# Column tiles for the attention scores of a cross-attention and expert kernel, with the value products moved behind them

## The reference, cut to what matters

```python
q = _ln(linear(ln_out, wq)).reshape(b, s, g, hpg, d)     # g = 8 groups, hpg = 2 heads each, d = 128
k = _ln(linear(ln_out, wk)).reshape(b, s, g, d)
v = linear(ln_out, wv).reshape(b, s, g, d)
scores = einsum('bsghd,btgd->bghst', q, k) * scale       # s = t = 64
core = einsum('bghst,btgd->bsghd', softmax(scores), v)
...                                                      # the same again with qx and with kx, vx of the context
out = einsum('bsi,oi->bso', quantized(concat(core, xout)), wproj)
x = x + out
x = x + experts(layernorm(x))
```

## Time and profile before

| | |
|---|---|
| median of 3 runs | 983.66 us (979.86 to 983.66) |
| span of the profiled execution, first to last instruction | 978.1 us |
| granted TensorE clock, mean | 0.996 |
| attention steps: scores at line 372 | 36.9 to 657.2 us |
| busy over the span: TensorE, VectorE, ScalarE, GpSimd | 97%, 82%, 75%, 47% |

### The profile page before, as it was taken

One profiled execution on the slowest core, in us unless ns is written; L12 is line 12 of the kernel. 1 busy time (PEld: TensorE's weight loads), 2 busy tenths in 40 slices (PEclk: granted clock), 3 DMA queues, 4 the chain that ended last, 5 costly groups with the idle time before them and its releaser, 6 DMA issues.

```text
span 978.1 us, 21551 instructions
## 1 busy us (share of the span) xinstructions
PE 946.2 (97%) x7240; PEld 674.7 (69%) x7240; DVE 798.2 (82%) x1720; ACT 736.5 (75%) x1370; POOL 458.5 (47%) x673
## 2 busy tenths in 40 slices
PE   5699999999999999999999999999999999999997
PEld 2476777777777777777777777776655566666665
DVE  6889999999999999999999999989799754444443
ACT  6988888888888888888888888865556645555554
POOL 5335655455465555555564655541036703333333
PEclk9999999999999999999999999999999999999999
DMA  9924201010001000100100010211558733343223
GB/s 220 330 73 87 44 23 55 23 47 26 28 29 45 28 28 23 49 29 22 50 23 28 28 45 28 72 65 55 182 166 241 232 114 50 50 70 57 44 29 38
DMA packets 36747, 70.35 MB, mean 72 GB/s; under 512 B 3617, under 2 KB 24737, under 8 KB 36513
## 3 DMA queue, kind: packets, MB, share of 16 engines
q1 hardware_dynamic: 27184, 54.39, 17.6%
q0 software_dynamic: 9456, 14.59, 8.8%
HBM read 55.52 MB, written 18.68 MB: 76 GB/s over the span
## 4 chain that ended last, share of the span: by engine, by line
PE 82%; DVE 9%; ACT 4%; issue 2%; POOL 1%; DMA 1%; POOLq 0%; DVEq 0%; ACTq 0%
PE b_pj L346 23%; PE b_sc L372 10%; PE b_tr L362 8%; PE b_o L401 7%; PE b_acc L444 5%; PE b_pj L1337 5%; PE b_o L1372 5%; PE b_o L1464 3%; PE b_pt L391 3%; PE b_tr L1337 3%; PE b_sc L1337 3%; PE b_pj L1417 2%; PE b_pt L1361 2%; PE b_sc L1417 1%; PE b_tr L1417 1%
## 5 line engine op out<-in xcount | busy, mean ns | idle before, releaser
L698 POOL TENSOR_TENSOR root<-vareps,neghalf 128x4 f32<-128x4 f32 (+1 forms) x128 | 174.2, 1361 | 10.0
L691 POOL TENSOR_TENSOR var<-ssq,unit 128x4 f32<-128x4 f32 (+1 forms) x128 | 54.4, 425 | 253.4 <-DVE ssq L524 253.4
L346 PE MATMUL b_pj<-w_hi,xq 128*128 128x512 f16 x384 | 147.9, 385 | 1.1 <-DVE xq L680 0.9
L346 PE MATMUL b_pj<-w_lo,xq 128*128 128x512 f16 x384 | 147.5, 384 | 0.0
L456 ACT ACTIVATE sq<-b_pj 128x512 f32<-128x512 f32 x192 | 114.9, 598 | 38.0 <-PE b_pj L346 35.0
L524 DVE TENSOR_REDUCE ssq<-sq 128x4 f32<-128x512 f32 x192 | 130.2, 678 | 9.4 <-ACT sq L456 9.4
L535 DVE TENSOR_TENSOR nrm<-raw,rstd 128x512 f32<-128x512 f32 x192 | 128.3, 668 | 1.6 <-POOL rstd L702 1.2
L372 PEld LDWEIGHTS b_sc<-kT,qT 128*128 128x128 f32 x1024 | 121.7, 192 | 6.1 <-ACT qT L483 1.7
L1313 POOL DMA_INDIRECT out<-xn x39 | 60.6, 1554 | 133.5 <-ACT xn L1543 124.0
L372 PE MATMUL b_sc<-kT,qT 128*128 128x64 f32 x1024 | 122.5, 273 | 0.7 <-ACT qT L483 0.7
L362 PE MATMUL b_tr<-ident,nrm 128*128 128x128 f32 x768 | 116.4, 274 | 6.8 <-DVE nrm L535 3.6
(11 more groups left out here) (327 smaller groups left out, 2271.7 us busy)
## 6 DMA issues: line engine op xcount, KB each, us to landing
nst<-in_ffw SPq DMA_DIRECT2D x40, 512.0 KB, 3.7
wload<-in_ffw SPq DMA_DIRECT2D x20, 512.0 KB, 4.5
xbuf<-zero SPq DMA_DIRECT2D x13, 387.0 KB, 9.7
xn<-xbuf SPq DMA_DIRECT2D x9, 516.0 KB, 3.7
x_sb<-in_x SPq DMA_DIRECT2D x4, 512.0 KB, 13.8
wproj<-in_ctxT SPq DMA_DIRECT2D x1, 2048.0 KB, 10.3
xhl<-in_w_all SPq DMA_DIRECT2D x4, 512.0 KB, 17.4
wproj<-in_wprojT POOLq DMA_DIRECT2D x4, 512.0 KB, 6.3
```

Of the source, the lines that this page charges most:

```text
L346: last = pe.matmul(o, x, w[kind][:, k, at:at + BANK], start=(k == 0 and n_ == 0), stop=(k == KT - 1 and n_ == len(terms) - 1))
L698: pool.tensor_tensor(root[:, r % 2, c, :], vareps[:, r % 2, c, :], neghalf[:, 0:1].unsqueeze(2).to_broadcast(shape), ALU.pow).then_inc(s[" ...
```

## The change

Each score product is split by head: 64 stationary columns of `qT` instead of 128, with the result on the partitions of that head (0 to 63 or 64 to 127) of the same columns of `b_sc`. A step has 16 such products instead of 8. In TensorE's list `pe_values` moves from behind the second transposes to the place right behind the scores. `pe_values` gets one more wait, in its first step only, for the last of the 32 weight units.

```diff
@@ pe_scores
                 for g in range(GU):
                     for b in range(2):
-                        last = pe.matmul(b_sc[:, (g * 2 + b) * S:(g * 2 + b + 1) * S], qT[:, r % 2, g * 2 + b, :],
-                                         kT[:, r % 2, g, b * S:(b + 1) * S], start=True, stop=True)
+                        for h in range(HPG):
+                            rows = slice(h * S, (h + 1) * S)
+                            last = pe.matmul(b_sc[rows, (g * 2 + b) * S:(g * 2 + b + 1) * S], qT[:, r % 2, g * 2 + b, rows],
+                                             kT[:, r % 2, g, b * S:(b + 1) * S], start=True, stop=True)
                 last.then_inc(s["sc_done"], 1)
@@ pe_values
                 after(pe, "cev_done", N)
+                if N == 0:
+                    pe.wait_ge(s["wlo_done"], len(UNITS))
@@ attention_tensor
                     (1, pe_scores, "scores"),
+                    (-1, pe_values, "values"),
                     (2, pe_transpose(0), "first transposes"),
                     (3, pe_project(0), "project 0"),
                     (0, pe_probT, "probT"),
                     (3, pe_project(1), "project 1"),
                     (2, pe_transpose(1), "second transposes"),
-                    (-1, pe_values, "values"),
                     (3, pe_project(2), "project 2"),
```

## The result

The changed kernel takes **973.76 us** (973.66 to 974.58, four runs) against 981.76 (979.75 to 983.66) for the kernel before on the same chip: a ratio of 0.992, 95% interval 0.990 to 0.994. It is faster by 0.8%, less than half of the 2% that was forecast, and the interval leaves out 1. The spans of the profiled executions are 972.9 and 978.1 us.

The account below looks back on a forecast made before the run. TensorE's list was taken to bound the kernel: 2.64 us shorter per four steps, 1.14 hidden by VectorE, so 14 x 1.50 = 21 us, less half a microsecond for rough edges, giving 963 us from 983.66. Range 948 to 1000 us.

Parts of the forecast that it names:

- What bounds the kernel: Attention steps: TensorE's own list sets the pace, busy 564.83 of 566 us, with VectorE near behind.
- What paces a score pass: Score products on TensorE: the weight load of 128 columns, not the product, sets the 0.108 us a pass.
- scores split by head: Score products: 32 half-width passes in two tiles side by side take 0.86 us a step instead of 1.73.
- One more change of mode: TensorE around the scores: entering their own tile shape costs 0.21 us a step; leaving stays 0.11.
- The move of the values: Values right behind the scores: later first transposes absorbed by ScalarE's 0.91 us idle; no cost counted.
- The new wait at N = 0: First step, wait for the last weight unit: cost nothing; some 2 us once if its cover were gone.
- VectorE is late next: Light steps: VectorE's 18.16 us floor for a pair hides 1.14 of the 2.64 us saved in four steps.
- VectorE does not cap it: Rival: VectorE's lag carries from light into heavy steps; 35 us less, 949 us; chance 0.08.
- loads in a queue: Rival, score products: half loads queue, 1.73 us a step plus 0.21 entry; 996 us; chance 0.14.
- the sequencer's pace: Rival, score products: no long run beats 0.068 us a pass, 2.18 a step; 1023 us; chance 0.04.
- load and product in turn: Rival, score products: each pass pays load and product in turn, 3.46 us a step; 1100 us; chance 0.08.
- the split changes little: Rival, scores: passes cost about 0.045 us, or modes 0.4 more than thought; 978 to 986 us; chance 0.08.

Follow-up runs that it names:

- e1: Changed kernel with the values back in their old place behind the second transposes, so only the scores are split: 956.56 us.
- e8: e1 with VectorE's square sums taken over half of the columns: 954.67 us.
- e4: Changed kernel with the loops turned, all score products of head 0 before those of head 1, so neighbours share a column tile: 1017.70 us.
- e2: Kernel before with only the values moved right behind the scores, scores still in 128 columns: 1013.65 us.
- e3: Changed kernel with the output projection moved ahead of the third transposes: 961.03 us.
- e7: Changed kernel with VectorE's three square sums taken over half of the columns: 972.43 us.
- e5: Changed kernel with ScalarE's exponential moved behind its second eviction, TensorE's list untouched: 978.53 us.
- e6: As e5, with VectorE's sum also moved behind its second square sum: 973.12 us.
- e9: Changed kernel with second transposes ahead of projection 1 on TensorE, ScalarE's second eviction right behind its copy of projection 0: 973.01 us.
- e11: As e9, but ScalarE's second eviction behind the exponential again, ahead of its square of projection 1: 964.16 us.
- e10: As e9, with VectorE's square sums taken over half of the columns: 953.19 us.

## Why the prediction was wrong

The sign and the range held; the size did not: 20.7 us were forecast (983.66 to 963), and the medians have moved by 8.0. By pairs of steps the miss lies in the heavy ones, 19.80 us where 18.70 was forecast; the light pair came out at 18.17 against 18.16, which was luck (point 6). By its own steps:

1. *What bounds the kernel.* Right: TensorE's list. It still sets the pace of e1 and e8, but for 0.28 us in four steps.
2. *What paces a score pass* and *scores split by head*: right. Predicted 0.86 + 0.21 = 1.07 us for a step, measured 1.08. Two column tiles of float32 work side by side, loads included, and e4 shows that the order of the instructions carries it (1.83).
3. *One more change of mode.* The entry was well enough sized within the 1.08, and from column to row tiles the values take 1.09 as before. Leaving the tiles was priced at 0.11 as today; with transposes behind them it is 0.15, 0.04 more a step. The second exit that the move saves is 0.11 a step, as the prediction had it.
4. *The move of the values*: **this is the step that failed.** It named the parts that the values pass and found room for their delay, but it priced only the parts that become later. It did not ask what the values had covered where they stood: the third transposes write the bank of the second ones, and in between ScalarE must get to the eviction and do it. The earlier trace rows had the values' 1.09 and the earlier trace rows ScalarE's first eviction; the second one was not looked at. Priced at 0, it measured 0.50 us a step in the timeline of the changed kernel, 0.46 against e1, and 0.57 alone (e2, 0.04 of exit in it). That is about 2.0 of the 2.6 us that TensorE's list was to get shorter in four steps, and e3 shows that the 0.87 us of the output projection in that place take the wait away.
5. *The new wait at N = 0*: its cost was covered. The scores that stand ahead of it start at 67.76 us (67.44 before) and the first values at 68.84, the 1.08 us that lie between the two in every step.
6. *VectorE is late next*: wrong in the changed kernel, and far too large for the split alone. The forecast floor of 18.16 us for a light pair was undercut by e1 with 8.72 + 8.90 = 17.62, and e7 and e8 didn't move with 0.8 us less VectorE work a step. The light pair of the changed kernel, 9.14 + 9.03 = 18.17, agrees with the floor by chance: it is TensorE's list, 18.34 less 1.30, with two waits of 0.50 and some 0.1 of exits. The error was to take the work between two maxima as bound to two light steps. In e1 the maxima start 2.13 us behind the scores at the start of the light pair (477.67 and 475.54) and 2.52 behind at its end (495.67 and 493.15); the heavy steps take that back. The rival "VectorE does not cap it" had said so, with a chance of 0.08, and for e1 it is the nearer one. What is left of the cap there is at most the 0.28 us around the wait for the norm, where 1.14 were forecast.

Of the other rivals, loads in a queue, the sequencer's pace and load and product in turn are all out: a run of 32 passes takes 1.08 us. The rule of the Trainium skill, page TensorE: Matmul & The Clock Gate, section Part 3: Packing small matmuls — row/col tiling, that a load overlaps running products only where row groups differ, does not hold for these column tiles, which share all rows: passes of 0.029 us are shorter than a load of 0.053 us alone. The same page of the Trainium skill, section Part 2: What happens when you issue a matmul, gives some 62 ns for each product where the hardware doesn't decode them. That pace is not seen here: 32 products in 1.08 us are 0.034 us each.

What happened in the changed kernel was "the split changes little" in its effect, but not in its reason: the split gave all it should, and the other half of the change took three quarters of it back.

Not settled: whether a better place for VectorE's norm would bring e1 its last 0.28 us in four steps, how e5 and e6 differ in detail in the light steps, and whether an order exists that keeps the cover without the second exit; e9 and e11 did not find it.

## What to carry to other kernels

When a part is moved in an engine's list, price both ends: what becomes late behind its new place, and which eviction or wait it covered at its old one. Two uses of one bank need other work between them as long as the whole way through the evicting engine, its place in that engine's list included. Here the third transposes could start 1.80 us after the end of projection 1 (485.28 to 487.08), and 1.30 us of work stood between. Products of half the array pay off when neighbours in the list sit in different tiles; try the split by itself first, and the saving of a mode change (0.11 us here) only where no cover is lost. When a chain runs through an engine, take some of its work away before calling it the cause: e7 did not move, e10 did.

## What was not expected of the hardware

Float32 products with 64 weight columns take about 0.053 us a pass (estimate in e4) when they follow each other in one column tile, and (1.08 - 0.15)/32 = 0.029 when two tiles alternate, loads included and for 32 passes on end. In these runs the cost of leaving the tiles goes by what comes next and not by the kind of tile: before float32 transposes 0.15 from column tiles (e1) and also 0.15 from row tiles (changed kernel, e2), before a float16 projection 0.11 from row tiles. Going from column tiles straight to row tiles added nothing that can be seen: the values behind the scores take 1.09 us, as before.
